# One transformer block on one core: the two ends of the program rebuilt, and two copies moved from ScalarE to VectorE

## The reference

```python
# attention: 16 heads of width 8, causal
q, k, v = split(xn @ w_in.T + b_in)
attn = softmax(mask(q * scale @ k.T));  o = attn @ v
a = o @ w_out.T + b_out
a = where(isnan(a), 0, a)
# ffn: 8 experts of width 176, the best 2 of each token, and a shared one of width 352
scores = softmax(xn @ gate_w.T);  combine = top2(scores), normalised, times 2.5
y = sum_e combine[:, e] * (silu(xn @ w_gate[e]) * (xn @ w_up[e])) @ w_down[e]  +  shared mlp
```

## Time and profile before

| what | value |
|---|---|
| median of 3 runs | 591.53 us (591.2 to 592.78) |
| the profiled execution's own time | 591.25 us |
| its span, first to last instruction | 589.3 us |
| granted TensorE clock, mean over the span | 0.977 |
| chain that ended last: PE, DVE, ACT, issue, POOL, DMA | 62%, 14%, 9%, 8%, 4%, 3% |

### The profile page before, as it was taken

One profiled execution on the slowest core, in us unless ns is written; L12 is line 12 of the kernel. 1 busy time (PEld: TensorE's weight loads), 2 busy tenths in 40 slices (PEclk: granted clock), 3 DMA queues, 4 the chain that ended last, 5 costly groups with the idle time before them and its releaser, 6 DMA issues.

```text
span 589.3 us, 13270 instructions
## 1 busy us (share of the span) xinstructions
PE 530.7 (90%) x4568; PEld 300.3 (51%) x4568; DVE 471.7 (80%) x826; ACT 342.2 (58%) x462; POOL 343.6 (58%) x365
## 2 busy tenths in 40 slices
PE   2657989998999999999999999999999999999893
PEld 2335642566436662467526663466525663366522
DVE  5967978899778988699777988699787989589513
ACT  5412379453893459634893459734794359734790
POOL 2165725576355864678356764578357773568442
PEclk9879999998999999999999999999999999999996
DMA  8894016900269004740169003850069003760001
GB/s 267 244 236 103 2 48 183 228 2 1 66 173 237 4 9 148 204 112 0 61 165 246 0 9 125 200 139 0 30 174 260 9 9 108 192 168 1 10 1 36
DMA packets 45613, 62.03 MB, mean 105 GB/s; under 512 B 4784, under 2 KB 29968, under 8 KB 45584
## 3 DMA queue, kind: packets, MB, share of 16 engines
q1 hardware_dynamic: 42876, 58.40, 37.6%
q10 hardware_dynamic: 2708, 3.24, 1.7%
HBM read 45.24 MB, written 15.34 MB: 103 GB/s over the span
## 4 chain that ended last, share of the span: by engine, by line
PE 62%; DVE 14%; ACT 9%; issue 8%; POOL 4%; DMA 3%; ACTq 0%; DVEq 0%; POOLq 0%
PE banks L620 11%; PE banks L483 7%; PE banks L518 7%; ACT probs L831 6%; PE banks L499 6%; PE banks L485 6%; PE banks L484 6%; PE banks L593 6%; DVE neg_max L1175 5%; PE banks L500 3%; PE banks L501 3%; DVE probs L1150 2%; POOL hid_lo L917 2%; DMA cb<-c_dram 2%; POOL probs L911 2%
## 5 line engine op out<-in xcount | busy, mean ns | idle before, releaser
L1175 DVE TENSOR_REDUCE neg_max<-banks 128x2 f32<-128x1024 f32 (+3 forms) x224 | 194.9, 915 | 17.9 <-PE banks L509 17.2
L955 POOL TENSOR_SCALAR_AFFINE_SELECT probs<-probs 128x512 f32<-128x512 f32 x128 | 91.7, 740 | 121.9 <-ACT probs L831 121.9
L831 ACT ACTIVATE probs<-banks 128x1024 f32<-128x1024 f32 x160 | 155.5, 1031 | 11.3 <-PE banks L593 9.0
L911 POOL TENSOR_TENSOR probs<-probs,cb 128x512 f32<-128x512 f32 x88 | 113.0, 1284 | 68.6 <-ACT probs L765 63.4
L765 ACT ACTIVATE probs<-banks 128x512 f32<-128x512 f32 (+1 forms) x112 | 66.8, 598 | 141.3 <-PE banks L485 140.6
L917 POOL TENSOR_TENSOR hid_lo<-probs,hid_hi 128x512 fp32r<-128x512 f32 (+1 forms) x88 | 114.6, 1303 | 42.4 <-ACT hid_hi L772 42.4
L483 PE MATMUL banks<-x_hi,w_hi 128*128 128x512 f32 (+1 forms) x224 | 94.6, 422 | 4.3 <-DVE w_lo L1352 2.2
L620 PE MATMUL banks<-probs,v_op 128*32 128x512 f32 (+3 forms) x1024 | 95.5, 445 | 0.6 <-POOL probs L955 0.4
L1150 DVE TENSOR_TENSOR probs<-probs,banks 128x512 f32<-128x512 f32 (+1 forms) x112 | 76.2, 680 | 24.4 <-POOL probs L911 17.9
L772 ACT ACTIVATE hid_hi<-probs 128x512 fp32r<-128x512 f32 (+1 forms) x96 | 60.4, 630 | 50.9 <-DVE probs L1150 50.6
L485 PE MATMUL banks<-x_hi,w_lo 128*128 128x512 f32 (+1 forms) x224 | 89.4, 399 | 0.0
(11 more groups left out here) (127 smaller groups left out, 577.8 us busy)
## 6 DMA issues: line engine op xcount, KB each, us to landing
q_op<-q_dram SPq DMA_DIRECT2D x16, 512.0 KB, 6.3
k_op<-k_dram SPq DMA_DIRECT2D x16, 512.0 KB, 7.8
cb<-c_dram SPq DMA_DIRECT2D x31, 256.0 KB, 4.5
cb<-c_dram SPq DMA_DIRECT2D x16, 224.0 KB, 4.8
q_dram<-q_parts SPq DMA_DIRECT2D x8, 384.0 KB, 2.6
k_dram<-k_parts SPq DMA_DIRECT2D x8, 384.0 KB, 2.6
cb<-c_dram SPq DMA_DIRECT2D x16, 192.0 KB, 4.7
cb<-c_dram SPq DMA_DIRECT2D x15, 160.0 KB, 4.8
```

The source lines that it names most:

```text
L831: nc.scalar.activation(probs[:, g % 2, 2 * u:2 * u + 2, :], ring[:, at:at + 2, :], ACT.Exp).then_inc(exp_done, 1)
L911: nc.gpsimd.tensor_tensor(sg[k % 3][:, :], sg[k % 3][:, :], cb[:, tiles_of(b)[k], :], ALU.mult).then_inc(weighted, 1)
L955: return nc.gpsimd.affine_select(out=view, in_=view, compare_op=ALU.is_ge, fill=0.0, base=0, pattern=[[0, 4], [1, P]], channel_multiplier=-1)
L1175: return nc.vector.tensor_reduce(out, in_, AX.X, ALU.max, negate=True)
```

## The change

- **Start.** VectorE now does the router's 13 steps of batch 0 and `take_combT` directly after `take_v`, then takes q itself, splits q and k, and only then meets tile 0. `low_routed(0)` moves behind tile 1, next to `low_routed(1)`. TensorE turns the router's weights before `gate_up` of tile 1. ScalarE sends them out after the silu of tile 1, ahead of a copy of `w_down`. SP no longer loads the output bias and `w_out` before q and k go out, but after the last router-weight loads. `PAIRS_FIRST` puts three pairs after each of the tiles 4 to 9 and two after tile 10 (before: three after 4 to 7, two after 8 to 11).
- **Every attention stage.** `take_q` and `take_y` run on VectorE. `transpose_y` moves from g = 0, u = 3 to g = 1, u = 1. `yT` lies in `o_sb`, so the exponential of unit 4 no longer waits for it.
- **Selection.** NaNs are dropped by `max(a, 0) + own` and `min(a, 0) + own`, two VectorE instructions, in place of the comparison, the predicated copy, GpSimd's clear and GpSimd's add.
- **End.** For batch 7 every step from `take_o` to the store is done in two halves of two token blocks each, each half in its own banks.

```diff
-PAIRS_FIRST = [3 * int(4 <= k <= 7) + 2 * int(8 <= k <= 11) for k in range(NT + 2)]
+PAIRS_FIRST = [3 * int(4 <= k <= 9) + 2 * int(k == 10) for k in range(NT + 2)]
@@ banks
-        yT = probs[:, 0, 8, :]
+        yT = o_sb[:, 0, :]
+        last_o = [banks[:, n, 0:S // 2] for n in (0, 1)]
+        last_on = [banks[:, n, 0:S // 2] for n in (2, 3)]
+        last_p = [banks[:, n, 0:S // 2] for n in (4, 7)]
@@ SP
             tokens_in(3)
-            sp.dma_start(bo_bc[:, :], b_o.partition_broadcast(P)).then_inc(out_weights, 16)
-            for j in range(4):
-                sp.dma_start(wo_sb[32 * j:32 * j + 32, :], ...)
...
             weights_around(2)
+            sp.dma_start(bo_bc[:, :], b_o.partition_broadcast(P)).then_inc(out_weights, 16)
+            for j in range(4):
+                sp.dma_start(wo_sb[32 * j:32 * j + 32, :], ...)
             maxima_in(0)
...
             store(NB - 2)
-            store(NB - 1)
-            sp.wait_ge(stored, 16 * NB)
+            for half_q in range(2):
+                rows = slice(half_q * S // 2, (half_q + 1) * S // 2)
+                at = (NB - 1) * QT + half_q * QT // 2
+                sp.wait_ge(last_summed, half_q + 1)
+                sp.dma_start(out[NB - 1, rows].rearrange("(q p) e -> p q e", p=P), x_sb[:, at:at + QT // 2, :]
+                             ).then_inc(stored, 16)
@@ TensorE
+            def last_transpose_o(n):
+                pe.wait_ge(last_taken, n + 1)
+                for at, q in last_blocks(n):
+                    mm = pe.transpose(last_o[n][:, at * P:(at + 1) * P], o_sb[:, 1, q * P:(q + 1) * P],
+                                      ident_sb[:, :])
+                mm.then_inc(last_back, 1)
...
+                    if k == 1 and i is None:
+                        transpose_comb(0)
                     if k < NT and (k >= 2 or i is None):
                         gate_up(b, k)
...
-                    if k == 2 and i is None:
-                        transpose_comb(0)
...
-                        if (g, u) == (0, 3):
+                        if (g, u) == (1, 1):
                             transpose_y(i)
...
-            transpose_o(NB - 1, 1)
-            transpose_on(NB - 1)
-            project_out(NB - 1)
+            for half_q in range(2):
+                last_transpose_o(half_q)
+            for half_q in range(2):
+                last_transpose_on(half_q)
+            for half_q in range(2):
+                last_project(half_q)
@@ ScalarE
                     if i is None and k == 1:
+                        weights_out()
                         high_routed_down()
...
-                    if i is None and k == 2:
-                        weights_out()
...
-                        if g == 0 and u == 4:
-                            act.wait_ge(yback_ready, i + 1)
...
-                        if (g, u) == (0, 1):
-                            take_y(i)
...
-                            if (g, u) == (0, 2):
-                                take_q(i + 1)
...
-            act.wait_ge(onT_ready, NB)
-            nc.scalar.activation(o_normT[:, :], nat[:, 0, :], ACT.Copy).then_inc(onT_done, 1)
+            for half_q in range(2):
+                cols = slice(half_q * S // 2, (half_q + 1) * S // 2)
+                act.wait_ge(last_turned, half_q + 1)
+                nc.scalar.activation(o_normT[:, cols], last_on[half_q], ACT.Copy).then_inc(last_turned_taken, 1)
@@ GpSimd
-                    if not (isinstance(i, int) and i == 0):
-                        add_clean(i - 1)
-                    clear(i)
...
-            add_clean(NB - 2)
-            clear(NB - 1)
@@ VectorE
+            def take_q(j):
+                dve.wait_ge(q_ready, j + 1)
+                nc.vector.tensor_scalar(qk_f[:, 0, :], nat[:, 0, :], QSCALE, bq_scaled[:, 0:1], ALU.mult, ALU.add
+                                        ).then_inc(q_done, 1)
+
+            def take_y(i):
+                dve.wait_ge(down_done, NT * i + NT)
+                nc.vector.tensor_copy(yT[:, :], bank_y[:, :]).then_inc(y_taken, 1)
...
+            def add_numbers(i):
+
+                own = x_sb[:, bass.ds(i * QT, QT), :]
+                dve.wait_ge(tail_step, 2 * i + 1)
+                nc.vector.scalar_tensor_tensor(out=own, in0=att[:, :, :], scalar=0.0, in1=own,
+                                               op0=ALU.max, op1=ALU.add).then_inc(tail_step, 1)
+                dve.wait_ge(tail_step, 2 * i + 2)
+                nc.vector.scalar_tensor_tensor(out=own, in0=att[:, :, :], scalar=0.0, in1=own,
+                                               op0=ALU.min, op1=ALU.add).then_inc(summed, 1)
...
-                    if k == 1 and i is None:
-                        router_weights(0)
                     if k == 2 and i is None:
-                        take_combT(0)
+                        low_routed(0)
                         low_routed(1)
...
                     split_k(i + 1)
+                    take_q(i + 1)
+                take_y(i)
+                if front:
                     split_q(i + 1)
...
-                    find_numbers(i - 1)
-                    finish_output(i - 1)
+                    add_numbers(i - 1)
...
-            low_routed(0)
+            dve.wait_ge(consts_loaded, 16 * 5)
+            router_weights(0)
+            take_combT(0)
+            dve.wait_ge(const_made, 1)
+            take_q(0)
             split_q(0)
             split_k(0)
...
-            take_o(NB - 1, 1)
-            normalise_o(NB - 1, 1)
-            add_attention(NB - 1)
-            find_numbers(NB - 1)
-            finish_output(NB - 1)
-            add_last()
+            for half_q in range(2):
+                last_take_o(half_q)
+            for half_q in range(2):
+                last_normalise_o(half_q)
+            for half_q in range(2):
+                last_output(half_q)
```

More of the change, by code:

```diff
@@ L539, in scores @@
                 elif i is not None and n == ONE_SLOT:
-                    pe.wait_ge(tail_step, 3 * i + 1)
+                    pe.wait_ge(tail_step, 2 * i + 1)
                 else:
@@ L868, in _ @@
             exp_router(0)
-            act.wait_ge(const_made, 1)
-            take_q(0)
             take_k(0)
@@ L938, in experts @@
                         place_v(b, i)
-            def clear(i):
-                before(pool, summed, i)
-                apart(pool, pool_passed)
-                nc.gpsimd.memset(clean[:, :, :], 0.0).then_inc(cleared, 1)
-            def add_clean(i):
-                own = x_sb[:, bass.ds(i * QT, QT), :]
-                pool.wait_ge(tail_step, 3 * i + 3)
-                nc.gpsimd.tensor_tensor(own, own, clean[:, :, :], ALU.add).then_inc(summed, 1)
             def mask(view):
```

84 lines of the change are left out of this document (52 added, 32 removed).

## The result

| | before | after |
|---|---|---|
| median of the runs beside each other (20 and 20) | 591.64 us (590.19 to 592.78) | 592.65 us (592.14 to 594.5) |
| the profiled execution's own time | 591.25 us | 593.64 us |
| its span | 589.3 us | 591.9 us |
| granted TensorE clock over the span | 0.977 | 0.979 |

The ratio after to before is 1.0021, with a 95% interval of 1.0012 to 1.003. The prediction was 588.2 us in a range of 584.3 to 591.0: wrong. The change costs about 1.2 us where 3.3 were to be won.

A forecast was written before the change was run, and what follows sets the result against it. TensorE (busy 90%) and VectorE (80%) bound the kernel, so savings count only where one waits. 591.25 - 2.3 (start) + 1.75 (attention stages) - 2.8 (end) = 587.9, with 0.3 for the median 588.2 us, range 584.3 to 591.0.

The forecast's parts named there:

- VectorE waits for TensorE right after them in either case: Selection in the attention stages: VectorE's two new steps, 0.69 us each, are followed by a wait for TensorE anyway.
- The change touches nothing there that TensorE waits for: Expert stages of the middle batches: TensorE runs almost without a gap and the change adds or saves nothing, 0 us.
- The start: From kernel start to VectorE's unbroken maxima: 2.3 us gained, bounds 1 us lost and 5 gained.
- The operand loads are issued 1.8 later too: Start: loads of q and k as operands go 1.8 us later, k at about 30.6, landing at 36.9.
- VectorE's three pairs after tile 4 run from 37.4: Start: VectorE begins these pairs at 37.4 us and needs 3.6 us, then `hidden` of tiles 3 and 4 follow.
- my chain: Start: after the pairs at 37.4, TensorE makes tile 5's products at 41.8; VectorE's next pairs start at 44.9 or 43.7.
- the start gains nothing: Rival, start: splits end 3.9 us later and operands replace cb as the late transfer; 590.5 us, chance 0.2.
- The attention stages: Eight stages, 1.75 us lost: unit 3 gains 0.46, y's turn adds 0.6; +0.14 each in the middle, +0.45 first, +0.4 last.
- late weights: Rival, attention stages: masks delay the router's weights, TensorE waits, each stage loses 1.0 us; 594.4 us, chance 0.08.
- The end: Last batch's output in halves, from VectorE's first copy to the last step: 2.8 us gained, bounds 2.0 and 3.5.
- at the slow clock as before: End: TensorE's projection takes 2.07 us for four blocks, so 1.04 us a half, with the slow clock assumed.
- the bound of 3.5: End: the upper limit of the gain, 3.5 us, if TensorE keeps its fast clock.

The follow-up runs named there:

- p_select: The kernel before with only the selection by max and min, in the change's place in the order; 592.34 us, ratio 1.0026.
- s_wait: p_select with one wait more: the second selection step (min) starts only after the GpSimd mask that TensorE waits for; 589.42 us, ratio 0.9975 to the kernel before.
- a_wait: The whole change with one wait more: the second selection step starts only after the GpSimd mask that TensorE waits for; 589.9 us, ratio 0.9981 to the kernel before.
- p_start: The kernel before with only the new start, q's first copy left on ScalarE; 591.12 us, ratio 1.0001.
- r_cb_late: p_start with the first group's weights loaded behind k's parts, by SP in place of ScalarE; 591.13 us, ratio 1.0 to the kernel before.
- b_bo: b_best with two edits of the change's start, the late loads of the output weights and the new `PAIRS_FIRST`; 586.96 us, ratio 0.9928 to the kernel before.
- b_best: The kernel before with the last output in halves and the selection by max and min with the wait on the mask; 587.46 us, ratio 0.9931.
- copies_t10: p_copies with y turned one unit earlier, at g = 1, u = 0; 594.1 us, ratio 1.0045 to the kernel before.
- q_copies_yfirst: The kernel before with q and y copied by VectorE, y ahead of k's split and turned in its old place; 594.41 us, ratio 1.0063.
- p_copies: The kernel before with only q's and y's copies on VectorE, batch 0's q too, and y's turn at g = 1, u = 1; 593.1 us, ratio 1.0037.
- a_q0: The whole change with batch 0's q copied by ScalarE as before; 593.15 us, ratio 1.0019 to the kernel before.
- y_only: The kernel before with only y's copy on VectorE, ahead of k's split, and y turned in its old place; 591.97 us, ratio 1.0012.
- p_tail: The kernel before with only the last batch's output in halves, with its selection by max and min there; 587.0 us, ratio 0.9937.

## Why the prediction was wrong

**The step that failed first: "VectorE waits for TensorE right after them in either case".** With that sentence, and with "The change touches nothing there that TensorE waits for" on the expert stages, I put the selection at nothing. VectorE does wait there, 1.85 us in p_select, and each step took the 0.69 I gave it. What I left out is what the step does beside itself. I had shown that a split step takes 1.00 instead of 0.69 beside a mask, and asked only what GpSimd does to VectorE, not what VectorE does to GpSimd. The price is 0.47 us in each of six expert stages, 2.8 in all; shown by s_wait and a_wait, where one wait takes it away. The Trainium skill ("SBUF — State Buffer", the section "SBUF: two separate sides") says that whichever of a VectorE instruction with two SBUF inputs and a GpSimd instruction that reads SBUF starts first has the shared pair for its whole length. The trace agrees on who loses, in both directions: the mask 0.07 us behind takes 1.11 for 0.64, and a_wait's step, behind the second mask, takes 1.10 for 0.69. The losses, 0.47 and 0.41 us, are shorter than the 0.62 and 0.55 that the other still had to run. I cited this rule in the prediction, for the other edit.

**The start: -2.3 forecast, nothing measured** (p_start 1.0001). The bookkeeping of VectorE was right to 0.1 us up to the splits. Then two steps failed. "The operand loads are issued 1.8 later too" was 3.9, because k's parts took 4.5 to 5.2 us to land beside the first weights instead of 3.2; I had counted less competition and there was more, one transfer earlier. The crowding is shown by r_cb_late, which also shows that it does not matter. The second was "VectorE's three pairs after tile 4 run from 37.4": they began at 40.06 in the change, on k_op, and at 39.27 and 39.26 in p_start and r_cb_late, where VectorE was busy until then. I had looked for what TensorE and GpSimd wait for and not for VectorE's own queue, into which I had moved `low_routed(0)`. From there my chain took 7.5 us to the next pairs and the trace 7.98, so they began at 48.04 and not at 44.9. With k's operands at TensorE at 36.3, 37.8 or 38.6 us, and cb at 36 or 40, the second set of maxima starts between 46.85 and 47.36, and the first exponential comes at 81.03 to 81.21 (b_bo, r_cb_late, p_start and before). Single profiles of a start lie up to 4 us apart, so that agreement is partly luck; the medians carry the point, p_start at 1.0001, r_cb_late at 1.0 and b_bo beside b_best. Which engine holds the start differs: TensorE's wait for k_op, `normalise` on VectorE, the weighed tile, ScalarE's wait for a landing. I have shown that it is held on several sides, not what the least of them is. The rival "the start gains nothing" (590.5) was the right one for this part.

**The attention stages: right.** +0.15 forecast and +0.18 measured for stages 1 to 6, and the working held: unit 3 is 0.38 us early (0.46), the turn then costs more than that, and copies_t10 shows the same cost in the other place of group 1. In its old place it costs nothing, as the prediction had it: stage 7 of q_copies_yfirst takes 19.65. Stage 0 lost 0.11 for 0.45 in the change and 0.17 in p_copies. Stage 7 lost 0.41 in p_copies (0.4 forecast); the change's profile has 1.94 there, for this reason, the granted clock:

```profile
564.00:567.40 3.40, 3.40 (x18) 0.99 (x22) 0.00 (x0) 2.40 (x3) 1.52 (x3) 0.51 0.00 0
```

The same stage took 20.26 in a_q0 and 20.28 in a_wait, so this 1.5 us belongs, as far as these two show, to one execution. So does the -0.68 of the first expert stage: before and all other kernels have a drop of the clock there, this execution has none. p_copies is 1.0037, 2.2 us, and its attention stages explain 1.7 of them and the last expert stage 0.28. The rest, 0.2, is within the interval.

**The rival "late weights"** did not occur in the change, and y_only shows that it was close: there TensorE waits 0.46 us for them and the stage is 20.65.

**The end: -2.8 forecast, -4.09 in the profile**, -3.7 by p_tail's ratio. The mechanism was right, the size was off by 1.3 us in the profile. The largest term is the projection, which I priced at 1.04 a half "at the slow clock as before". In both halves together it took 1.20, for the clock stays at 1.0 until 591.3 us. Before, it fell at 579.0. With the turns ahead of it, also shorter than I took them, that is 0.7 of the 1.3. I had named the fast clock as the bound of 3.5 and not taken it. Another 0.5 is the last store: I had written that its wait of 2.3 us comes again, and for half the size it was 1.83.

```profile
573.80:579.00 5.20, 3.48 (x36) 0.89 (x29) 2.26 (x5) 1.00 (x2) 4.06 (x5) 1.00 0.08 23
579.00:589.30 10.30, 3.19 (x12) 2.49 (x12) 3.17 (x5) 0.60 (x1) 0.00 (x0) 0.50 0.14 39
```

These are the tail before and after the fall, with the columns as above. The old tail itself depends on it: in p_copies, whose last instructions are those of before, the clock fell 7.4 us behind the last exponential instead of 5.2, and the tail was 14.65 us instead of 15.53. Against that the halves gain 3.2. The clock fell 5.2 to 7.4 us behind the last exponential in all eleven profiles with the whole tail, and 9.4 to 11.8 in all seven with the halves, so the later fall comes with the halves. That it comes because TensorE's gaps are shorter there is argued, not shown.

**The sum.** By the ratios: tail -3.7 us, selection in the expert stages +2.6 (1.5 measured alone, with its tail gain of 1.1 inside), copies +2.2, start 0: +1.1, measured +1.2. My range ended at 591.0, and its upper end held one failed term, not two.

## What to carry to other kernels

An edit that costs its own engine nothing can still lengthen its neighbour: before moving a VectorE instruction with two SBUF operands into a gap, look which GpSimd instruction starts there and who waits for it; if the order is unlucky, one wait for the critical one was enough here. Cut both traces at an instruction that recurs in each stage, for the shares of busy time hide 0.47 us six times over. And of a start that is full of transfers, free no single wait without asking, engine by engine, what is in each queue at the moment of the gain; and judge it by medians, as one profile of the same start lay anywhere in 4 us.

## What the runs showed of the hardware

- A GpSimd mask of 128x512 that started 0.07 us behind a VectorE instruction with two SBUF inputs took 1.11 us instead of 0.64; a predicated copy that started 0.25 us behind the mask left it at 0.64 and took 0.99 itself, where one with GpSimd idle took 0.73 (the end of the kernel before).
- `scalar_tensor_tensor` on 128x512 float32 took 0.68 us with GpSimd idle and 0.69 when it started ahead of a mask, 1.01 to 1.11 when a mask had started before it, and 0.42 on 128x256. `tensor_tensor` took 0.69 and 0.42.
- The three writes of k's parts, 128 to 384 KB, landed 3.1 to 3.3 us after issue with no weight load beside them (r_cb_late), and 4.8 to 5.2 us beside three loads of 96 to 256 KB issued by another engine (p_start).
- A write of 16 KB was waited for 2.0 to 2.4 us when it was issued 0.2 us or more ahead of a load of 512 KB, and 4.0 to 5.6 us when it was issued about with it or behind it.
- The granted clock fell 5.2 to 7.4 us behind the last exponential in all eleven profiles with the whole tail, and 9.4 to 11.8 us behind it in all seven with the halves.
- One and the same start ran with a granted clock between 0.72 and 0.93 from 36 to 60 us in different executions, and its first exponential came 4.2 us apart.
